# Between the two steps of a graph layer: another order for loads, transposes, logits and the first two searches

## The reference

```python
h = relu(layernorm(x))
S = adj + eye
Rf = S / S.sum(axis=1, keepdims=True)
Rb = S / S.sum(axis=0)[:, None]
Xf = Xb = Xa = h
for s in range(2):
    logits = (Xa @ W1) @ W2 @ (Xa @ W3).T
    # per row: keep the largest logits until their softmax sums to 0.9
    A = softmax(where(keep, logits, -inf))
    Xf, Xb, Xa = Rf @ Xf, Rb @ Xb, A @ Xa
    Z = Z + Xf @ U1[s] + Xb @ U2[s] + Xa @ U3[s]
x = x + layernorm(h + Z) * gamma + beta
```

## Time and profile before

| | |
|---|---|
| median of 3 runs | 2369.52 us (2368.68 to 2369.74) |
| the profiled execution | 2369.85 us, span 2368.1 us |
| busy in the span | PE 2154.2, DVE 2057.3, ACT 1939.9, POOL 731.0 us |
| mean granted clock of TensorE | 0.970 |
| end of the first loop, start of `third(0)` on PE | 956.58 us |
| start of the second loop's `start_search(1)` and `start_search(2)` on DVE | 1195.64 and 1240.86 us |

### The profile page before, as it was taken

How to read it: one execution, slowest core, us unless ns; L and a number is a source line. 1 busy time by engine, 2 the same in 40 slices (tenths; PEclk the granted TensorE clock), 3 DMA queues, 4 the chain that set the end, 5 groups by cost and what they waited for, 6 DMA issues and landing times.

```text
span 2368.1 us, 26066 instructions
## 1 busy us (share of the span) xinstructions
PE 2154.2 (91%) x8250; PEld 1380.8 (58%) x8250; DVE 2057.3 (87%) x3825; ACT 1939.9 (82%) x2849; POOL 731.0 (31%) x987
## 2 busy tenths in 40 slices
PE   7599999999999998899799999999999999999975
PEld 4377767776777767443355555555555555555454
DVE  5699999999999998134989999999999999999995
ACT  5899999999999995236578988988989889889834
POOL 2133443344333442001123223233232232332332
PEclk9699999999999999999899999999999999999997
DMA  7245444555445452332222112112121221121242
GB/s 245 82 112 131 110 106 100 123 116 115 94 112 122 110 110 52 102 98 41 46 61 55 39 50 57 37 51 55 51 43 50 51 57 36 50 57 40 53 116 70
DMA packets 85166, 190.03 MB, mean 80 GB/s; under 512 B 12193, under 2 KB 65056, under 8 KB 85024
## 3 DMA queue, kind: packets, MB, share of 16 engines
q0 software_dynamic: 26208, 61.37, 16.5%
q1 hardware_dynamic: 56496, 125.48, 16.0%
q10 hardware_dynamic: 2320, 1.48, 0.2%
HBM read 154.19 MB, written 34.10 MB: 80 GB/s over the span
## 4 chain that ended last, share of the span: by engine, by line
DVE 46%; PE 22%; ACT 17%; issue 6%; POOL 5%; DMA 0%; SPq 0%; DVEq 0%; ACTq 0%; POOLq 0%
DVE junk L1869 16%; PE bank L1144 10%; ACT junk L1431 6%; DVE logits L2036 6%; DVE small L1913 4%; DVE logits L1905 4%; DVE small L1811 4%; POOL small L1700 3%; DVE small L1796 3%; PE bank L1118 2%; PE bank L1134 2%; PE bank L753 2%; ACT logits L1324 2%; ACT junk L1390 2%; PE bank L776 2%
## 5 line engine op out<-in xcount | busy, mean ns | idle before, releaser
L1869 DVE SCALAR_TENSOR_TENSOR junk<-logits,small,expd 128x3327 uint8<-128x3327 f32 x184 | 677.9, 3684 | 4.8
L1118 PE MATMUL bank<-both,pair 128*128 128x512 f32 x1352 | 612.8, 598 | 26.4 <-ACT sides L1474 25.4
L1144 PE MATMUL bank<-h_aug,turns 128*128 128x256 f32 x2704 | 634.4, 381 | 1.5 <-ACT turns L1453 1.5
L1144 PEld LDWEIGHTS bank<-h_aug,turns 128*128 128x128 f32 x2704 | 496.6, 190 | 106.5 <-issue 24.9
L1118 PEld LDWEIGHTS bank<-both,pair 128*128 128x128 f32 x1352 | 250.8, 190 | 313.2 <-issue 260.8
L1118 PE MATMUL bank<-h_aug,both 128*128 128x257 f32 x1352 | 335.4, 397 | 29.5 <-ACT sides L1460 28.5
L1118 PEld LDWEIGHTS bank<-h_aug,both 128*128 128x128 f32 x1352 | 258.5, 197 | 112.9 <-ACT sides L1460 48.9
L1684 POOL TENSOR_TENSOR small<-small 128x1 f32<-128x1 f32 x52 | 14.8, 285 | 899.6 <-DVE small L1938 895.5
L1390 ACT ACTIVATE junk<-expd,small 128x3327 int8<-128x3327 f32 x88 | 270.4, 3072 | 3.0 <-POOL small L1679 2.7
L1384 ACT ACTIVATE junk<-expd,small 128x3327 int8<-128x3327 f32 x88 | 270.1, 3069 | 1.5
L1102 PE MATMUL bank<-KTr,QT 64*128 64x512 f32 (+1 forms) x728 | 232.6, 616 | 20.4 <-ACT logits L1324 16.5
(11 more groups left out here) (250 smaller groups left out, 2981.9 us busy)
## 6 DMA issues: line engine op xcount, KB each, us to landing
both<-adj_turned SPq DMA_DIRECT2D x52, 832.0 KB, 6.9
both<-adj_turned POOLq DMA_DIRECT2D x52, 832.0 KB, 11.0
pair<-adj_turned SPq DMA_DIRECT2D x52, 832.0 KB, 4.5
z<-sides POOLq DMA_DIRECT2D x52, 128.0 KB, 3.2
spread<-sides POOLq DMA_DIRECT2D x26, 128.5 KB, 3.7
turns<-spread SPq DMA_DIRECT2D x26, 128.5 KB, 2.1
attended<-att_out SPq DMA_DIRECT2D x26, 128.0 KB, 1.7
expd<-attended SPq DMA_DIRECT2D x26, 128.0 KB, 2.1
```

The source lines that it names most:

```text
L1118: done = pe.matmul(SX[:, 0:width], half(t, h)[:, bass.ts(jj, P)], rows_of(j), start=(j == 0), stop=(j == T - 1))
L1144: last = pe.matmul(AB[:, 0:D], attT[i % 4][:, b, :], h_aug[:, g + b, 0:D], start=(g + b == 0), stop=(g + b == T - 1))
L1869: chain.did(dve.scalar_tensor_tensor(junk[:, 0:N], logits[t % 3][:, 0:N], col(t, "cand"), expd[t % NE][:, 0:N], ALU.is_gt, ALU.mult, accum ...
```

## The change

It takes the same computation in another order in and around the middle:

- **Weights late.** `load_rest` is issued by SP in its iteration 6 of the loop over attended tiles, behind `load_att(14)`, not ahead of `load_att(6)`.
- **Eight ahead.** Eight attended tiles are loaded, turned and stored before the loop. `turn_att(0)` to `(5)` and their stores move into iteration 25 of the first loop (between the products of tile 24). Queries have a bank of their own (`QB`); keys 0 and 1 and queries 0 are made before the kept row of tile 25 is turned.
- **Logits in pairs.** The 14 chunks of tiles 0 and 1 alternate between banks 2 and 4, two at a time: four chunks in the last iterations of `third`, ten in slots 0 to 4. The sum and the fold of the keys move into the loop of `third` (iterations 21 and 23).
- **Spread tiles two ahead.** `turn_spread`, `store_spread` and `invert` run two tiles ahead. The parts `spread(0, n)` begin at slot 5.
- **Searches.** `row_max(0)` comes after two slots, `row_max(1)` after five; the whole search of tile 1, `keep(0)` and `row_max(2)` are placed among and behind the slots; the second loop begins on DVE with `start_search(2)`. On ACT `square` moves to iteration 16 of `third`, and `count_ties(0)` and `lift(0)` to slots 16 and 17.
- `z_out` lies in `sides`, no longer in `row_buffers[2]`, so `read_sides(0)` and `(1)` wait for the last adds of the buffers that they write over, and `own(0)` for the first loop's stores.

```diff
-        z_out = [row_buffers[2][:, 4 * KT * D + i * D:4 * KT * D + (i + 1) * D] for i in range(4)]
+        z_out = [sides[:, (i + 2) % 4 * D:((i + 2) % 4 + 1) * D] for i in range(4)]
+        QB = banks[4]
@@ SP, middle
         for t in range(T):
-            if t == 0:
+            if t + 8 < T:
+                sp.wait_ge(first.sem[f"att_stored{t % 2}"], 16 * ((t + 8) // 2 + 1))
+                parts.load_att(t + 8)
+            if t == 6:
                 sp.wait_ge(first.sem["kept_ready"], T + 1)
                 parts.load_rest()
-            if t + 6 < T:
-                ...
-                parts.load_att(t + 6)
             if t > 0:
                 parts.store_own(t - 1)
@@ PE, logits of tiles 0 and 1
-                if i > 0:
-                    pe.wait_ge(sem["logits_stored"], i)
+                if i > 1:
+                    pe.wait_ge(sem["logits_stored"], i - 1)
@@ PE, middle
-        parts.make(wq2, "queries", 0)
+        parts.make(wq2, "queries", 1)
         pe.wait_ge(first.sem["att_read"], T)
         for t in range(T):
             parts.third(t)
-            if t + 6 < T:
-                parts.turn_att(t + 6)
-            if t % 4 == 2 and (t + 2) // 4 < NG:
-                parts.make(wk2, "keys", (t + 2) // 4)
-            if t % 4 == 3 and (t + 1) // 4 < NG:
-                parts.make(wq2, "queries", (t + 1) // 4)
+            if t + 8 < T:
+                parts.turn_att(t + 8)
+            g = t // 4 + 1
+            if t % 4 == 0 and 1 < g < NG:
+                parts.make(wk2, "keys", g)
+            if t % 4 == 1 and 1 < g < NG:
+                parts.make(wq2, "queries", g)
+            if t == T - 3:
+                ... (fold of the keys)
+            if t == T - 2:
+                pe.wait_ge(mid["queries_stored"], NG)
+                make_logits(0, (0, 1))
+            if t == T - 1:
+                make_logits(0, (2, 3))
         parts.turn_spread(0)
+        parts.turn_spread(1)
         for t in range(T):
-            if t + 1 < T:
-                parts.turn_spread(t + 1)
+            if t + 2 < T:
+                parts.turn_spread(t + 2)
             parts.products(t)
-            if t < 2 * NC:
-                make_logits(t // NC, (t % NC,))
-            if t % 4 == 0 and t > 0:
+            for i in range(4 + 2 * t, min(6 + 2 * t, 2 * NC)):
+                make_logits(i // NC, (i % NC,))
+            if t % 4 == 1 and t > 1:
                 spread(0, t // 4 - 1)
@@ PE, iteration 1 of the second loop
+            if t == 1:
+                make_logits(2, range(4))
+                spread(1, 0)
+                make_logits(2, range(4, NC))
+                spread(1, 1)
@@ ACT, middle
-        slots(0, 8)
+        slots(0, 3)
         exponentials(0)
-        slot(8)
+        slot(3)
         guess(0)
+        slot(4)
+        probe(0, 0, lambda: slot(5), lambda: slot(6))
+        probe(0, 1, lambda: slot(7), lambda: slot(8))
         slot(9)
-        ...
+        exponentials(1)
+        slot(10)
+        guess(1)
+        slot(11)
+        probe(1, 0, lambda: slot(12), lambda: slot(13))
+        probe(1, 1, lambda: slot(14), lambda: slot(15))
         slot(16)
+        count_ties(0)
         slot(17)
+        lift(0)
@@ POOL, middle: prepare(0), prepare(1), count_needed(0), settle(0) after add_own(2), (9), (15), (16)
@@ DVE, middle
+        slots(0, 2)
         row_max(0)
-        slots(8, 14)
+        slots(2, 5)
+        row_max(1)
+        slots(5, 8)
         start_search(0)
-        ...
+        slot(8)
+        for k in range(late):
+            bisect(0, k)
+            slot(9 + k)
+        threshold(0, lambda: slot(14))
+        sum_larger(0)
         slot(15)
+        start_search(1)
         slot(16)
+        bisect(1, 0)
         slot(17)
+        bisect(1, 1)
         slot(18)
+        keep(0)
         slot(19)
+        bisect(1, 2)
+        slots(20, T)
+        bisect(1, 3)
+        row_max(2)
+        bisect(1, 4)
+        threshold(1)
+        sum_larger(1)
-    for t in range(0 if first_step else 1, T):
+    for t in range(0 if first_step else 2, T):
```

More of the change, by code:

```diff
@@ L736, in make @@
                 pe.wait_ge(mid["att_kept"], t + w)
-                if target == "queries":
-                    pe.wait_ge(mid["keys_stored"], g + 1)
-                elif g > 0:
-                    pe.wait_ge(mid["queries_stored"], g)
+                if g > 0:
+                    pe.wait_ge(mid[target + "_stored"], g)
+                bank = KQ if target == "keys" else QB
                 for k in range(KT):
-                    last = pe.matmul(KQ[:, 0:w * P], weights[:, k, :], xTg[g % 2][:, k, 0:w * P],
+                    last = pe.matmul(bank[:, 0:w * P], weights[:, k, :], xTg[g % 2][:, k, 0:w * P],
                                      start=(k == 0), stop=(k == KT - 1))
@@ L1050, in sync @@
                             sp.wait_ge(sem["kept_ready"], T - 1)
-                            for n in range(4):
+                            for n in range(8):
                                 sp.wait_ge(sem[f"att_stored{n % 2}"], 16 * (n // 2 + 1))
@@ L1078, in sync @@
                     if first_step:
-                        for n in (4, 5):
-                            sp.wait_ge(sem[f"att_stored{n % 2}"], 16 * (n // 2 + 1))
-                            parts.load_att(n)
                         store_attended(T - 1)
@@ L1214, in tensor @@
                         if first_step and not present:
-                            pe.wait_ge(sem["logits_stored"], T * copied)
-                            pe.wait_ge(sem["logits_taken"], T * (NC - copied))
-                            for n in range(4):
-                                parts.turn_att(n)
-                            parts.turn_att(4)
-                            parts.turn_att(5)
-                            parts.make(wk2, "keys", 0)
+                            parts.make(wk2, "keys", 0)
+                            pe.wait_ge(sem["spread_read"], T)
+                            parts.make(wq2, "queries", 0)
+                            parts.turn_att(6)
+                            parts.turn_att(7)
+                            parts.make(wk2, "keys", 1)
                         if not present and not first_step:
@@ L1596, in scalar @@
                             if not present:
-                                for n in range(6):
-                                    parts.store_att(n)
                                 parts.store_keys(0)
+                                parts.store_queries(0)
+                                parts.store_att(6)
+                                parts.store_att(7)
+                                parts.store_keys(1)
                             if following:
@@ L1612, in scalar @@
                                 read_spread(t)
+                            if t == T - 1:
+                                for n in range(6):
+                                    parts.store_att(n)
                             if previous:
@@ L1617, in scalar @@
                                 read_sides(t - 1)
+                            if t > 1 and present:
                                 count_ties(t - 1)
@@ L2065, in vector @@
                     else:
+                        pad = keys_of(NG - 1, NP - (NG - 1) * 512)[:, N - NP:]
+                        for i in range(2):
+                            dve.wait_ge(first.sem[f"spread_stored{i}"], 16 * (T // 2))
                         for t in range(T):
                             parts.own(t)
-                        pad = keys_of(NG - 1, NP - (NG - 1) * 512)[:, N - NP:]
-                        dve.wait_ge(mid["keys_stored"], NG)
-                        chain.did(dve.tensor_tensor(fold[:, :], ident[:, 0:DA], ident[:, DA:P], ALU.add))
```

142 lines of the change are left out of this document (75 added, 67 removed).

## The result

The changed kernel takes 2348.36 us (median of 4 runs, 2347.8 to 2350.41), the kernel before 2369.1 us (4 runs, 2367.58 to 2369.74): a ratio of 0.9915, with a 95% interval of 0.9898 to 0.9932. The forecast was 2351.5 us in a range of 2343.5 to 2361.5. The profiled execution took 2348.52 us, with a span of 2346.7.

The account below looks back on a forecast made before the run. VectorE was taken to bound the second loop, neither engine the middle. `start_search(2)` 19.4 us earlier, less 1.2 for `keep(1)`, took the profiled 2369.85 us to 2351.7, or 2351.5 as median; 8-in-10 range 2343.5 to 2361.5.

Parts of the forecast that it names:

- Six attended tiles into iteration 25: End of the first loop: with six turns moved there, `third(0)` begins 1.2 us later, at 957.8.
- The loop of `third`: Loop after the first: 64.1 us of passes, fold 0.3, two logits pairs 2.3; no wait for the keys' sum.
- Weights late: Loop of `third`: the stall for the tile behind the weights shrinks to 3.3 us, plus 1.9 of slow clock: 5.2.
- Slots 0 to 8: Behind the loop of `third`: `exponentials(0)` 17.2 us in, then 29.5, so `start_search(0)` after 46.7, at 1076.4.
- VectorE full to 1153.3: Slots 8 to 21: VectorE runs without waits, 76.9 us from `start_search(0)` to the first half of `gather(19)`.
- The tail is TensorE's: Slots 20 to 25: TensorE sets the pace, to 1181.4, with `products(21)` slow at 5.3 us.
- ACT's chain to `start_search(2)`, VectorE idle 13 us: Before `start_search(2)`: it waits for ACT until 1221.5, 19.4 us earlier than before; the idle time holds the remaining gain.
- After it: Start of the second loop: `keep(1)` waits 1.2 us more for ACT's `count_ties(1)`, leaving 18.2 us of gain.
- B: Rival: weights hidden in the loop of `third` and no slow products at 1153, 2344.5 us; chance 0.13.
- C: Rival: weights stall as long as before and VectorE waits for ACT in a few slots, 2361 us; chance 0.19.
- D: Rival: TensorE stays at the low clock level from slot 9 on, 2376 us; chance 0.04.
- E: Rival: the change moves nothing, the gain falling under 4.7 us; chance 0.04.

Follow-up runs that it names:

- e8: Changed kernel with each slot's two logits chunks parted, one between the halves of `products` and one behind them: 2353.39 us.
- e9: Changed kernel with the sum of the keys, its fold and the first two logits pairs put back behind the last `third`: 2352.89 us.
- e3: Changed kernel with the part of tile 1's search among slots 15 to 19 moved behind slot 25, in VectorE's list only: 2341.87 us.
- e5: Changed kernel with tile 0's search steps two slots apart and `keep(0)` and tile 1's search behind slot 25; ACT's and GpSimd's lists follow: 2330.07 us.
- e1: Changed kernel with the weights issued at iteration 0, ahead of the attended tile, as in the kernel before: 2354.85 us.
- e2: Changed kernel with the weights issued by GpSimd's queue, right after the first loop's last keep, instead of SyncE's: 2344.66 us.
- e4: Changed kernel with ACT running `exponentials(2)` ahead of the first store of turned tiles in the second loop: 2348.25 us.
- e10: e6 with slot 8 ahead of `start_search(0)`, the first step behind slot 9, and threshold, `count_ties(0)`, `lift(0)` and GpSimd's counting a slot later: 2325.07 us.
- e11: e6 with tile 0's search steps behind slots 9, 11, 13, 15 and 17, and slots 21 and 22 inside the threshold: 2323.66 us.
- e12: The changed kernel run again without any edit: 2348.85 us.
- e7: Changed kernel with spread tiles turned, stored and their row sums inverted one ahead of `products` instead of two: 2349.36 us.
- e6: Changed kernel with the edits of e2 and e5 together: 2325.12 us.

## Why the prediction was right, by its own steps

- **Six attended tiles into iteration 25.** `third(0)` was put at 957.8 and came at 954.91 and 956.76; kernels with the same first loop spread over 3.4 us (954.87 to 958.27). A term of 1.2 us can't be read from one execution; it is neither shown nor refuted. Of the work taken out of the loop, two makes are fewer in it, not three; the 3.9 us are the sum with two.
- **The loop of `third`.** 71.9 us forecast, 72.2 in the trace (954.91 to 1027.08). Pairs: right, and shown by e8. Sum of the keys: no wait, and 3.4 us by e9, where I had counted the 2.5 of the wait.
- **Weights late.** A stall of 3.3 and 1.9 of slow clock forecast; 3.4 and about 1.7 in the trace, and only 3.1 and 3.2 with no slow clock in e3 and e5. e1 gives back what the step gains; e2 shows the cause, SyncE's list.
- **Slots 0 to 8.** `start_search(0)` 46.7 us after the loop forecast, 46.6 in the trace: 17.7 to `exponentials(0)` and 28.9 from there, where 17.2 and 29.5 were forecast.
- **VectorE full to 1153.3.** 76.9 us forecast, 76.8 in the trace (1073.66 to 1150.46). Here the description was right and its meaning missed. The trace then said that TensorE waited 17.4 us in seven places; the forecast had only slow `products(21)` (5.3 us; they took 3.5). e3 and e5 show what this order costs: 6.5 and 18.3 us in the time. e3 edits VectorE's list alone; in e5 ACT's and GpSimd's lists moved with it, and no run parts the two.
- **The tail is TensorE's.** 28.1 us from the first half of `gather(19)` to the logits of tile 2 forecast, 26.4 in the trace (1150.46 to 1176.82): the 1.8 of the slow products are the difference. In e2 they were slow (5.30) and the tail as long as forecast: the term is real and comes and goes with the clock.
- **ACT's chain to `start_search(2)`, VectorE idle 13 us.** 13.1 in the trace. From the logits of tile 2 to `start_search(2)` it took 41.0 us, where 40.1 were forecast. The chain as drawn was right; that it was where the rest of the gain stays was half right, as e4 shows: without it the next wait, for TensorE's logits of tile 3, is as long.
- **After it.** `keep(1)` was to wait 1.2 us more. This step was wrong: it waits 0.3, as `keep(2)` does in the kernel before, 7.6 us after the start of the search in both, so the term is nothing. `row_max(3)` waits 0.2. In return 1.3 us went behind that: from `start_search(3)` to the end of the span are 1083.9 us before and 1085.2 after. e1, e3, e9, e10 and e11 have 1083.9 to 1084.2, the other runs 1085.1 to 1085.6, both profiles of the changed kernel among them. None of these edits touches that stretch; what decides between the two values stays open.

The middle was forecast at 263.7 us (957.8 to 1221.5) and measured at 262.9 and 263.4. The profiled execution was forecast at 2351.7 us and took 2348.52; 2.9 of these 3.2 us are the start of `third(0)`, which differs from execution to execution; in e12's profile, where it came at 956.76, the time was 2350.97. The medians (2348.36 and 2348.85) are 3.1 and 2.7 below the forecast, and of their other executions no trace shows the start.

Of the 21 us, e1 takes back 5.0 (weights), e8 5.0 (five pairs) and e9 3.4 (sum of the keys) ahead of `start_search(0)`, and e7 nothing. The rest was not undone in a run: the work moved ahead of the loop (3.9 us by the forecast's sum), and the new places of the searches against those of the kernel before.

**The rivals.** B would have shown no wait for the tile behind the weights; it has to be made by another queue (e2). The forecast held for B that U is small against Wq and Wk; it is not, with four DMAs of 256 KB against two of 512. C asked for waits of VectorE for ACT in the probes: there are none between 1073.66 and 1160; the 17.3 us of waits for `store_products` lie before and behind that. D took TensorE to the low level from slot 9 on: the clock was 0.91 in that stretch, and behind three of the seven waits the eight passes of `products` took 5.3 to 5.9 us instead of 3.6. By the forecast's count it begins to cost below 0.69. (The prediction gives the page's rule the time of "the last rival"; E stands last, but only D has the low level, so D is meant.) One of each kind:

```profile
1120.80 5.85 PE L776 MATMUL bank<-logits,turns 128*128 128x512 f32 x8 [4.46 <-DVE sides L854]
...
1143.98 3.67 PE L776 MATMUL bank<-logits,turns 128*128 128x512 f32 x8 [2.65 <-DVE sides L854]
```

The Trainium skill (TensorE: Matmul & The Clock Gate, HAM oscillation) describes a loop that is throttled again at every wait, its bursts of matmuls being shorter than its waits. Here a burst is 3.4 us at full clock and only the wait of 4.46 us is longer. The passes behind it were slow, as they were behind the 6.2 us at the same place in e1, e2, e3 and e8 (rows of 5.21 to 6.65 us): so far the traces agree. Behind shorter waits both happened: at 1091.11 a wait of 2.66 us was followed by 5.34 us of passes, at 1143.98 one of 2.65 by 3.67; a wait of 1.96 us was followed by 3.67 in e5 and by 5.37 in e6. What decides is not shown. About 6 us of TensorE's time went to it in the changed kernel, but in the stretch that VectorE paces they cost the kernel nothing, as e1 shows. E fell with the first row of the result.

## What to carry to other kernels

Two nearly full engines share a stretch: give the one that runs ahead of the next stage its pace first, and put the other's long operations between, as thinly as the buffers between them ask (here two slots for each step of 4.3 us). Filling idle time early with work that has a later hole is no gain, and can cost time: 15.8 us of VectorE's work, begun early, cost 6.5 us. The busy share of the engine that was filled looks best in the slower kernel, so count what the other engine waits for it. Ask of a load that comes late whether its bytes or its place in an in-order queue is the cause; a queue with nothing behind it, and the time of issue of the late load in both traces, settle that in one run.

## What the hardware showed besides

The issue of one DMA can hold a queue far longer than another of the same size: Wqs and Wks, 512 KB each, took SyncE 0.47 and 3.65 us back to back, and GpSimd 1.19 and 1.18. Why is not shown.

GpSimd's small operations can take as long as the scan that VectorE runs beside them. In the changed kernel's first loop:

```profile
900.80 3.69 DVE L1910 SCALAR_TENSOR_TENSOR junk<-logits,small,expd 128x3327 uint8<-128x3327 f32 x1
```
```profile
900.90 3.63 POOL L1721 TENSOR_SCALAR small<-small 128x1 f32<-128x1 f32 x1
...
932.87 0.19 POOL L1721 TENSOR_SCALAR small<-small 128x1 f32<-128x1 f32 x1
```

The same line takes 3.63 us as the scan begins just ahead of it, and 0.19 without one. The Trainium skill (SBUF — State Buffer, Who interferes with whom) has it that a VectorE instruction with two inputs in SBUF contends with a GpSimd instruction that reads SBUF. The rows agree. It lies on the path: the chain of what ended last runs through the 3.63 us above, and VectorE's next `keep` waits for the end of GpSimd's list:

```profile
907.40 0.16 DVE L2070 RECIPROCAL small<-small 128x1 f32<-128x1 f32 x1 [2.35 <-POOL small L1743]
```

In the second loop it is L1736 that takes 3.3 us beside the first scan of the search, and `keep` waits 0.3 us in each of 24 tiles, 7.2 us in all. No run moves GpSimd's operations out of the scans, so what that would gain is open.
